# Message stage: the multiply by scale moves from VectorE to GpSimd, and Exp and Ln name one activation table set

## The reference

```
z = concatenate([h[src], h[dst], edge_feats], axis=1)
gate = sigmoid(batchnorm(z @ W_int + b_int))
upd  = softplus(batchnorm(z @ W_upd + b_upd))
agg  = segment_sum(gate * upd, dst)
out  = softplus(h + batchnorm(agg))
```

## Time and profile before

| | us |
|---|---|
| median of 3 runs | 11238.83 |
| lowest and highest run | 11232.6, 11250.45 |
| span of the profiled execution (first to last instruction) | 11234.0 |
| message stage in it, about | 4252 to 5213 |

### The profile page before, as it was taken

One profiled execution on the slowest core, in us unless ns is written; L12 is line 12 of the kernel. 1 busy time (PEld: TensorE's weight loads), 2 busy tenths in 40 slices (PEclk: granted clock), 3 DMA queues, 4 the chain that ended last, 5 costly groups with the idle time before them and its releaser, 6 DMA issues. The chain is left out here.

```text
span 11234.0 us, 448798 instructions
## 1 busy us (share of the span) xinstructions
PE 8366.9 (74%) x151748; PEld 7090.9 (63%) x151749; DVE 8649.2 (77%) x21890; ACT 6257.6 (56%) x14808; POOL 5047.9 (45%) x5196
## 2 busy tenths in 40 slices
PE   6444444378889997996877788778887788777877
PEld 6444344278877777886756667467675576655855
DVE  6776667578889999998686785976868858679367
ACT  0222222169987777997405536975359863589410
POOL 1777777734430001111371471753726627356057
PEclk8555555589999998998999989999889998899999
DMA  6655553269989997996996998979989789897997
GB/s 220 185 179 183 180 168 90 70 215 330 331 281 259 258 248 261 322 322 210 329 328 247 290 271 301 312 248 288 272 285 316 242 302 272 274 322 256 373 326 264
DMA packets 1297726, 2929.45 MB, mean 261 GB/s; under 512 B 381368, under 2 KB 925682, under 8 KB 1272400
## 3 DMA queue, kind: packets, MB, share of 16 engines
q1 hardware_dynamic: 956540, 1976.18, 51.0%
q0 software_dynamic: 296704, 823.09, 24.7%
q10 hardware_dynamic: 44116, 125.96, 4.0%
HBM read 1753.54 MB, written 1104.99 MB: 254 GB/s over the span
## 5 line engine op out<-in xcount | busy, mean ns | idle before, releaser
L574 POOL DMA_INDIRECT rows_s<-place_rec,place_index x1568 | 1523.3, 971 | 531.0 <-issue 514.2
L665 PE MATMUL place_slot_ps<-place_runs,place_oh_turned 50*128 50x100 f32 x3136 | 728.5, 423 | 1072.5 <-ACT place_oh_turned L613 1025.6
L2959 POOL DMA_INDIRECT hop_x<-cols_all,hop_index x864 | 988.3, 1144 | 1024.1 <-ACT hop_index L2968 757.5
L665 PEld LDWEIGHTS place_slot_ps<-place_runs,place_oh_turned 50*128 50x128 f32 x3136 | 683.1, 327 | 1103.3 <-issue 1091.3
L2977 ACT ACTIVATE hop_parts<-hop_x,mask 128x64 f32<-128x64 f32 x5184 | 1258.7, 336 | 10.7 <-issue 6.6
L3024 PEld LDWEIGHTS hop_sums_ps<-hop_parts,hop_onehot 128*128 128x128 bf16 x18144 | 587.4, 97 | 650.6 <-issue 649.9
L1853 POOL DMA_DIRECT2D cm_onehot<-hot_d x288 | 152.7, 531 | 1774.4 <-POOLq L107 977.8
L3024 PE MATMUL hop_sums_ps<-hop_parts,hop_onehot 128*128 128x64 bf16 x18144 | 687.7, 193 | 334.2 <-DVE hop_parts L3006 321.5
L2764 POOL DMA_INDIRECT mask_cols<-cols_all,mask_index x432 | 432.6, 1001 | 790.9 <-ACT mask_index L2788 679.6
L2761 POOL DMA_INDIRECT mask_cols<-cols_all,mask_index x432 | 672.1, 1556 | 254.0 <-ACT mask_index L2788 162.7
L622 ACT COPY place_rec<-keys 128x32 f32 (+1 forms) x98 | 21.5, 219 | 1309.7 <-DMA place_rec<-in_e 1261.1
(11 more groups left out here) (498 smaller groups left out, 28533.6 us busy)
## 6 DMA issues: line engine op xcount, KB each, us to landing
cols_all<-att_in_rows SPq DMA_DIRECT2D x216, 896.0 KB
mask_onehot<-hot_s SPq DMA_DIRECT2D x108, 1792.0 KB
cols_all<-hop_in_rows SPq DMA_DIRECT2D x216, 896.0 KB
hop_onehot<-hot_s SPq DMA_DIRECT2D x864, 224.0 KB
rows_all<-blank SPq DMA_DIRECT2D x72, 1808.0 KB
ct_u<-rows_all SPq DMA_DIRECT2D x288, 452.0 KB
cm_v<-rows_all SPq DMA_DIRECT2D x288, 448.0 KB
cm_onehot<-hot_d POOLq DMA_DIRECT2D x288, 448.0 KB
```

The source lines that it names most:

```text
L574: nc.gpsimd.indirect_dma_start(m.rows_s.rearrange("p n w -> (p n) w"), bass.IndirectOffsetOnAxis(index[:, j, t:t + 1], 0), rec[:, j, t, :] ...
L665: last = nc.tensor.matmul(slot_ps[b][:, t, 0:2 * NBK], oh_turned[:, b, t, :], runs[:, b, t, :], start=True, stop=True)
L2959: nc.gpsimd.indirect_dma_start(x[:, n, :, :].rearrange("p c f -> p (c f)"), None, table, bass.IndirectOffsetOnAxis(index[:, n:n + 1], 0)). ...
```

## The change

`rescale` leaves VectorE's program. GpSimd's step, now unrolled by twelve, first issues its one-hot load and then does `rescale` for batch it+10 (before: it+8, on VectorE); ahead of its loop it does the first ten. `value` stays on VectorE, eight ahead. On ScalarE, `damp` names a table set, `natural_log_exp_and_others`, just before the Exp of each group. Nothing else changes.

```
 GpSimd:
+                def rescale(it, n, round):
+                    pool.wait_ge(u_came[n], round * 16 + 16)
+                    pool.sem_inc(gate, 1)
+                    nc.gpsimd.tensor_tensor(v[:, n, :, :], v[:, n, :, :], b2(scale[:], BATCH), ALU.mult).then_inc(scaled, 1)
-                def step(it, i, k, more, s):
+                def step(it, s, i, k, more, _):
+                    n = s * 4 + i
                     if look_ahead(it, 4):
                         pool.wait_ge(summed, it + 3)
                         load_hot(it + 4, i)
+                    if look_ahead(it, 10):
+                        rescale(it + 10, (n + 10) % 12, k + (n + 10) // 12)
                 for i in range(4):
                     load_hot(i, i)
-                each4(pool, step)
+                for n in range(10):
+                    rescale(n, n, 0)
+                each12(pool, step)
 ScalarE, damp:
                     act.sem_inc(gate, 1)
+                    nc.scalar.preload_act_table_set("natural_log_exp_and_others")
                     nc.scalar.activation(log[:, s, :, :, :], log[:, s, :, :, :], ACT.Exp, scale=-1.0).then_inc(damped, 1)
 VectorE:
-                def rescale(it, n, round):
-                    dve.wait_ge(u_came[n], round * 16 + 16)
-                    dve.sem_inc(gate, 1)
-                    nc.vector.tensor_tensor(v[:, n, :, :], v[:, n, :, :], b2(scale[:], BATCH), ALU.mult).then_inc(scaled, 1)
 step:
-                    if ahead:
-                        rescale(it + 8, (n + 8) % 12, k + (n + 8) // 12)
                     weigh(it, s, i, k)
 ahead of the loop:
                 for x in range(8):
-                    rescale(x, x, 0)
                     value(x, x)
```

## The result

| | before | after |
|---|---|---|
| median (us) | 11237.93 (5 runs) | 11556.43 (5 runs) |
| lowest, highest | 11220.58, 11250.45 | 11488.66, 11566.58 |
| span of the profiled execution | 11234.0 | 11487.1 |

The changed kernel is slower: the ratio is 1.0273, with an interval of 1.0259 to 1.0286. The forecast was 11,246, and its range ended at 11,540.

What follows compares the result with a forecast made beforehand. VectorE was taken as the bound at 3.20 us an iteration. Span 11234.0 + 8 (stage) - 1 (start) = 11241; with the median 4.8 above the span, 11246 us, range 11,185 to 11,540.

Steps and rivals of the forecast that it cites:

- The multiply at 2.08: Price of one 128x896 multiply on GpSimd, from nearest rows: 2.08 us, bounds 1.88 and 2.26.
- The exclusion: GpSimd's multiply and VectorE's max-and-add and product can't run beside each other; exclusive use 3.21 us an iteration.
- The forecast's pattern: Changed loop with max-and-add held at 1.3 us or more, product free at 0.62: 3.23 us an iteration.
- The start: Beginning of the stage: about -3.5 us, against +1 to +4 from first sums at half clock; counted as -1.
- both rings: Exclusive use by GpSimd and VectorE, 3.21 us; L1981 through TensorE's sums and GpSimd back to L1981, 3.19 an iteration.
- the +8 us of the sum: Stage's share of the forecast: 3.23 us against 3.20 before, over 278 iterations.
- the 0.60: Chance given to the forecast, with its own range 11,200 to 11,300.
- The slower rival: Multiply goes between L1972 and L1981, holding every second product: 4.15 us an iteration, +264 us, 11,505; chance 0.27.
- the slower sums: TensorE's 14 matmuls at half clock, 2.9 us in place of 1.75 once in two iterations: +160 us more.
- a race, 5.88 against 5.90: GpSimd's next multiply could be there at 5.88 us, L1981 asks for the ports at 5.90; the earlier goes first.
- The two rows: Evidence on ports: a VectorE instruction 0.45 us ahead of a GpSimd add was held; L1531, 0.15 ahead, wasn't.
- the faster rival: Ports matter less, or GpSimd wakes during its multiply: down to TensorE's 2.9 us, -83 us, 11,160; chance 0.13.

Runs made afterwards that it cites:

- the memset run: Changed kernel with a small GpSimd memset of 0.28 us between the one-hot issue and the multiply: 11598.74 us, ratio 1.0320.
- the two halves of 448: Changed kernel with GpSimd's multiply cut into two of 448 elements, back to back: 11583.7 us, ratio 1.0310.
- the kernel with two issues: Changed kernel with the one-hot load of each step issued as two DMAs: 11411.5 us, ratio 1.0152.
- the move alone: Changed kernel without the table edit, so only the multiply moves to GpSimd: 11530.42 us, ratio 1.0238.
- the split: Changed kernel with GpSimd multiplying only the update half and VectorE the gate half: 11153.24 us, ratio 0.9928.

## Why the prediction was wrong

**What held.** VectorE as the bound, with L1960 as the piece that leaves it. The multiply at 2.08 (2.10 measured), at a DMA share of 0.81 to 0.93 beside it. The exclusion: max-and-add held, the sum at 1.08 untouched. The forecast's pattern at 3.23 (3.26 over 72 iterations). The table edit at nothing on the kernel before. The start, counted as -1, was small, but the 5.6 us by which the first product came earlier don't confirm it, since kernels with both edits had it anywhere from 8.1 earlier to 0.9 later.

**The step that failed** is "The multiply asks at 3.16 after L1981's end, when the next L1981 (3.21) is just finishing, so both rings close", with the +8 us of the sum and the 0.60 laid on it. In place of the +8 the stage took +246.4. Those two rings describe one rhythm, in which GpSimd waits for TensorE's sums. The slower rival, at 4.15 an iteration and a chance of 0.27, is the other rhythm of the same program: when GpSimd's semaphores are already there, it doesn't wait, and its next multiply shuts out the product. The runs show that one at 4.22 for a full-clock pair of iterations and 4.32 on average. The range failed by a term as well: its upper end, 11,540, took in the rival at full clock (11,505) and left out the slower sums, which the rival had priced at up to +160. They occur in part of the stage, as the granted clock of 0.86 shows, and 4.32 over 278 iterations is 11,550 by the same sum, against the median of 11,556. That the price came so near is partly luck, since the rival had every second product held and the run one in three.

**Why its chance was too low.** I made it a race, 5.88 against 5.90, in which the earlier record wins. It wasn't close: measured between the records, the product needs a lead of 0.3 to 0.4 us. The two rows pointed in opposite directions, the held L3000 with a lead of 0.45 and the free L1531 with 0.15. L3000 looked like this case, a long two-operand instruction in front of a GpSimd instruction behind a DMA issue; L1531 stood in front of a copy of seven elements. I let the copy decide. The Trainium skill, "SBUF — State Buffer", section "SBUF: two separate sides", says that whichever of the two starts first gets the shared ports for its whole instruction; by record starts the memset run speaks against that, since the product began 0.08 earlier and lost, while "for the whole instruction" agrees with every row. The Trainium skill's "GPSIMD Engine Reference", Instruction dispatch, by which each core of GpSimd goes on to the next instruction when its own share is done, stood behind the rival, and the two halves of 448, with no turn for VectorE between them, agree with it.

**What I did not look for.** A ring that closes at 3.21 against a neighbour at 3.19 says nothing of what happens after a disturbance. The trace of before held one, the 5.34 us at 4646; a look at GpSimd's longest idle times would have found it. In the changed kernel it ends the good rhythm at product 111, and in the kernel with two issues each such pause starts a few held products. What brings the good rhythm about in the first place, at product 37 in this execution and never in the profiled one of the move alone, stays open. That the four slower executions of the changed kernel had no such stretch is argued only: 72 x (4.32 - 3.26) = 76 us is about their distance of 66 to 78 from the profiled one.

**Sizes.** TensorE's floor is 2.73, not 2.9: without the multiply its groups start 1.56 and 1.17 apart, and my 1.34 for the second was the length of its record, whose end overlaps the next group's start. With it the faster rival would be 11,234 - 0.47 x 287, about 11,100, which the kernel without the multiply has (11,099). The table edit is worth nothing while VectorE binds at 3.20, and 118 us once the split has taken the iteration to 2.95.

## What to carry to other kernels

Before work moves to GpSimd, list VectorE's instructions with both operands in SBUF, and give GpSimd no more than fits beside those that aren't. Where two engines share something exclusively, don't ask only whether a rhythm closes, but which one the loop falls into after a late instruction: here GpSimd, once its semaphores were always there, took the turn of about one product in three. A removed cost that is worth nothing now should be tried again once the bound has moved.

## What the runs showed of the hardware

- VectorE got no turn between two GpSimd multiplies issued back to back: one 128x448 product was held through both, 2.55 us in place of 0.62, its record counting as busy. Whoever reads VectorE as 91% busy in the changed kernel has to compare mean lengths by line.
- A message product (both operands in SBUF) that began outside a multiply was held in every case with a lead of 0.29 us or less on a GpSimd multiply of 896 elements, and ran free in every case with 0.40 or more; between 0.30 and 0.39 both occur.
- GpSimd paused some 2.7 us beyond its wait once in about 110 DMA issues of its own, at its issues 113 and 223 of the stage (from 0) with one an iteration, in the kernel before too, and every 108 issues, 54 iterations, with two. Its cause is open.
- The DMA engines moved 377 GB/s at a busy share of 1.14 where TensorE was the bound, after 323 at 0.97 before.
